# Last layer of a convolution and Fourier chain: two pairs of images side by side, inverse transform in halves, stores per image

## What is computed

```
z = conv3x3(x, Kj)                    # "conv1"
z = relu(batchnorm(z))                # statistics over all images
z = conv3x3T(z, Kj)                   # "conv2"
x = x + 0.1 * z
x = batchnorm(x)                      # statistics over all images
x = real(ifft2(fft2(x) * t))          # t: a table per channel and frequency
```

## Time and profile before

| | us |
|---|---|
| median of 3 runs | 667.3 (663.94 to 668.04) |
| the profiled execution, its own time | 662.35 |
| its span | 660.5 |

### The profile page before, as it was taken

The page is one execution under the profiler, slowest core; times in us unless marked ns, Lnnn a source line. Parts: engine busy times, 40 slices in busy tenths (PEclk is TensorE's granted clock), DMA queues, the critical chain, the costliest instruction groups (busy, mean ns, idle before and its releaser), DMA issues.

```text
span 660.5 us, 14557 instructions
## 1 busy us (share of the span) xinstructions
PE 616.0 (93%) x5848; PEld 196.2 (30%) x5848; DVE 499.6 (76%) x946; ACT 300.8 (46%) x518; POOL 236.7 (36%) x183
## 2 busy tenths in 40 slices
PE   6598999989999999999999999999999999999883
PEld 4122333322323232223232222333322223333331
DVE  3679888876588877668887967689879676887674
...
GB/s 188 192 167 123 34 34 25 24 53 66 218 52 2 1 66 66 66 193 174 2 1 63 5 73 87 229 110 1 1 66 66 66 108 216 2 1 2 0 66 191
DMA packets 44466, 51.21 MB, mean 78 GB/s; under 512 B 36208, under 2 KB 36336, under 8 KB 42352
## 3 DMA queue, kind: packets, MB, share of 16 engines
...
## 4 chain that ended last, share of the span: by engine, by line
PE 82%; DVE 10%; issue 3%; ACT 1%; DMA 1%; SPq 1%; POOL 0%; DVEq 0%; ACTq 0%; POOLq 0%
PE psum L1124 47%; PE psum L1201 7%; PE psum L1274 5%; PE psum L1348 5%; PE psum L1305 4%; PE psum L1333 3%; DVE work L1025 3%; PE psum L1152 2%; PE psum L1330 2%; PE psum L1189 2%; PE psum L1232 1%; PE psum L1234 1%; DVE work L852 1%; DVE work L1060 1%; DVE spare L852 1%
## 5 line engine op out<-in xcount | busy, mean ns | idle before, releaser
L1124 PE MATMUL psum<-Z,wts 128*32 128x512 f32 x1536 | 173.2, 595 | 0.0
L1124 PE MATMUL psum<-X,wts 128*32 128x512 f32 x1536 | 171.9, 594 | 0.1
L493 POOL TENSOR_TENSOR Z<-X 128x512 f32<-128x512 f32 x64 | 81.9, 1303 | 219.2 <-DVE X L1001 218.1
L584 ACT ACTIVATE Z<-psum 128x512 f32<-128x512 f32 x64 | 38.1, 595 | 114.9 <-PE psum L1124 103.8
L512 POOL TENSOR_TENSOR X<-Z 128x1024 f32<-128x1024 f32 x24 | 57.0, 2398 | 88.2 <-DVE Z L1042 88.2
L648 ACT ACTIVATE Z<-Z,small 128x512 f32<-128x512 f32 (+4 forms) x92 | 80.3, 922 | 4.5 <-DVE small L964 4.0
L1124 PEld LDWEIGHTS psum<-X,wts 128*32 128x32 f32 x1536 | 46.5, 109 | 113.7 <-issue 110.2
L1124 PEld LDWEIGHTS psum<-Z,wts 128*32 128x32 f32 x1536 | 45.7, 109 | 112.6 <-issue 111.0
L870 DVE BATCH_NORM_STATS2 stats<-Z 128x6 f32<-128x512 f32 x60 | 41.1, 689 | 43.6 <-ACT Z L584 43.2
L669 ACT ACTIVATE work<-X,small 128x512 bf16<-128x512 f32 x64 | 45.5, 713 | 59.1 <-DVE X L1001 59.1
L1001 DVE SCALAR_TENSOR_TENSOR X<-psum,X 128x512 f32<-128x512 f32 x64 | 43.6, 682 | 24.1 <-PE psum L1124 22.7
...
## 6 DMA issues: line engine op xcount, KB each, us to landing
...
```

The source lines that it names most:

```text
L493: nc.gpsimd.tensor_tensor(rows(Z0, REG, bp, CH * (2 * half + i), CH), low, high, op=op)\
L1124: last = nc.tensor.matmul(out_b[C * r:C * r + C, :], weights[:, o:o + C], rows(src, reg, bp, g, CH, dj - 1), start=(dj == 0), stop=(dj == ...
```

## The change

It has four parts.

1. In the last layer, the `fwdW` of pair 2 is no longer done behind `conv2` chunk 14. It stands in the tail, right before the `fwdW` of pair 3, and then both pairs pass `slot0`, `fwdH`, `invH` one after the other, each step of pair 2 followed by the same step of pair 3, instead of pair 3 following pair 2 at a distance. The `invW` and `back` of pair 1 come first in the tail, ahead of `moments`. Pair 3 gets buffers of its own for `turned`, `freqw` and `spec`, cut out of X2, which nobody reads any more by then.
2. `invH` of pairs 0 to 2 of the last layer is done in halves as in the other layers (with weights of their own, 128 more columns in `cst`, 64 KB), and POOL does `unmix_halves` for them; `affine` reads its result from X0. Pair 3 keeps the dense form.
3. A store is one DMA per image and half of a pair, from all 128 partitions, 256 KB, issued after each half's `affine`, for pairs 0 to 2. Pair 3: also one DMA per image and half. 16 DMAs in all where there were 20.
4. `affine` of pairs 0 and 1 comes after `slot0c` of pair 3; `affine` of pair 2 waits for POOL, and stands ahead of `affine` of pair 3 in ACT's order.

```diff
@@ -44,7 +44,9 @@
 C_STACK = C_MASK + 2
 C_QUAD = C_STACK + C
 C_FH = C_QUAD + R
-C_ALL = C_FH + 64
+C_IB = C_FH + 64
+C_ALL = C_IB + 128
+BY_HALVES = 3
 P_K = 0
 P_F = P_K + 2 * TAPS * C
...
@@ -137,7 +139,7 @@
         11: fourier(j, 1, "fwdH") + [("slot0c", j, 1)],
         12: fourier(j, 0, "invW") + [("back", j, 0, 0), ("back", j, 0, 1)],
         13: fourier(j, 1, "invH"),
-        14: fourier(j, 2, "fwdW"),
+        14: fourier(j, 2, "fwdW") if j + 1 < DEPTH else [],
     }
     for c in range(NCH):
         steps.append(("conv2", j, c))
...
@@ -171,12 +173,14 @@
 def last_steps(j):
-    steps = [("slot0", j, 2)] + fourier(j, 2, "fwdH") + [("slot0c", j, 2), ("moments", j)]
-    steps += [("turn", j, BP - 1, 0), ("turn", j, BP - 1, 1), ("norm", j, 2), ("affine", j, 0)] + fourier(j, 3, "fwdW")
-    steps += fourier(j, 2, "invH") + [("slot0", j, 3)] + fourier(j, 3, "fwdH") + [("slot0c", j, 3)]
-    steps += fourier(j, 1, "invW") + [("back", j, 1, 0), ("back", j, 1, 1), ("affine", j, 1)]
-    steps += fourier(j, 2, "invW") + [("back", j, 2, 0), ("back", j, 2, 1)] + fourier(j, 3, "invH") + fourier(j, 3, "invW")
-    return steps + [("affine", j, 2), ("back", j, 3, 0), ("back", j, 3, 1), ("affine", j, 3)]
+    steps = fourier(j, 1, "invW") + [("back", j, 1, 0), ("back", j, 1, 1), ("moments", j)]
+    steps += [("turn", j, BP - 1, 0), ("turn", j, BP - 1, 1)] + fourier(j, 2, "fwdW") + fourier(j, 3, "fwdW") + [("norm", j, 2)]
+    for bp in (2, 3):
+        steps += [("slot0", j, bp)] + fourier(j, bp, "fwdH") + [("slot0c", j, bp)]
+    steps += [("affine", j, 0), ("affine", j, 1)] + fourier(j, 2, "invH") + fourier(j, 3, "invH")
+    for bp in (2, 3):
+        steps += fourier(j, bp, "invW") + [("back", j, bp, 0), ("back", j, bp, 1), ("affine", j, bp)]
+    return steps
 SUMS = {c: (c,) for c in range(3)} | {4: (3,), 6: (4,), 9: (5, 6), 10: (7, 8), 11: (9,), 12: (10, 11), 13: (12, 13), 14: (14,), 15: (15,)}
...
@@ -352,6 +356,21 @@
                 return pool_slot[pool_product(c, dj, r) % POOL_SLOTS]
             return dve_slot[dve_product(c, dj, r) % DVE_SLOTS]
+        def beside(j, bp, t, i):
+
+            return X2[:, WORK * i:WORK * (i + 1)] if (j, bp) == (DEPTH - 1, BP - 1) else t[:, :]
+
+        def rows_of(j, bp):
+            return beside(j, bp, freqw, 0)
+
+        def spectrum(j, bp):
+            return beside(j, bp, spec, 1)
+
+        def turned_half(j, bp, half):
+            if (j, bp) == (DEPTH - 1, BP - 1):
+                return X2[:, 2 * WORK + 2 * N * half:2 * WORK + 2 * N * (half + 1)]
+            return turned[(2 * bp + half) % 3]
+
         block = ctx.enter_context(nc.Block())
         class Bank:
...
@@ -394,12 +413,17 @@
                     to = lines(t, reg, bp, a, b - a, 0, C * q, C * q + C).rearrange("p (g b) w -> p b g w", b=2)
                     eng.dma_start(to[:, b2], in_dram(x_in, 2 * bp + b2, r)[:, a + dg:b + dg]).then_inc(done, 16)
-        def store(eng, bp, l, n):
-
-            for q in range(R):
-                to = out[2 * bp:2 * bp + 2].rearrange("i c (q l) w -> q c i (l w)", q=R)[q]
-                both = Z2[C * q:C * q + C, bp * REG2:bp * REG2 + 2 * G * W].rearrange("p (i x) -> p i x", i=2)
-                eng.dma_start(to[:, :, W * l:W * l + W * n], both[:, :, W * l:W * l + W * n]).then_inc(out_done, 16)
+        def store(eng, bp, h, first=0, n=G):
+
+            for b2 in range(2):
+                if bp < BY_HALVES:
+                    to = out[2 * bp + b2].rearrange("c (h q l) w -> h q c (l w)", h=2, q=R)[h]
+                    o = bp * REG2 + (2 * b2 + h) * 2 * CH * W
+                    eng.dma_start(to, Z2[:, o:o + 2 * CH * W]).then_inc(out_done, 16)
+                else:
+                    to = out[2 * bp + b2].rearrange("c (q l) w -> q c (l w)", q=R)[:, :, W * first:W * (first + n)]
+                    o = bp * REG2 + b2 * G * W + W * first
+                    eng.dma_start(to, Z2[:, o:o + W * n]).then_inc(out_done, 16)
         def shift_two(eng, dst, src, bp, done, h=None):
...
@@ -452,11 +476,12 @@
                     sp.dma_start(parS[:, :], par[j + 1]).then_inc(par_in, 16)
             for bp in range(BP - 1):
-                sp.wait_ge(x_back, NCH * (DEPTH - 1) + Q * bp + Q)
-                store(sp, bp, 0, G)
+                for h in range(2 if bp < BY_HALVES else 1):
+                    sp.wait_ge(x_back, NCH * (DEPTH - 1) + Q * bp + (2 * h + 2 if bp < BY_HALVES else Q))
+                    store(sp, bp, h)
             sp.wait_ge(x_back, NCH * DEPTH - Q + 2)
-            store(sp, BP - 1, 0, G // 2)
-            sp.wait_ge(out_done, 16 * R * (BP + 1))
+            store(sp, BP - 1, 0, 0, G // 2)
+            sp.wait_ge(out_done, 16 * 2 * (BP + 1 + BY_HALVES))
         @block.gpsimd
         def _(pool):
...
@@ -508,7 +533,8 @@
                 pool.wait_ge(x_summed, NCH * j + Q * bp + Q)
                 even, odd = (rows(Z0, REG, bp, 2 * CH * p, 2 * CH).rearrange("p g (b w) -> p g b w", b=2) for p in range(2))
                 for half, op in enumerate((ALU.add, ALU.subtract)):
-                    dst = rows(X0, REG, bp, 2 * CH * half, 2 * CH).rearrange("p g (w b) -> p g b w", b=2)
+                    dst = rows(X0, REG, bp, 2 * CH * half, 2 * CH)
+                    dst = dst.rearrange("p g (b w) -> p g b w" if j == DEPTH - 1 else "p g (w b) -> p g b w", b=2)
                     nc.gpsimd.tensor_tensor(dst, even, odd, op=op).then_inc(parts_added, 1)
             for j in range(DEPTH):
...
@@ -521,7 +547,7 @@
                         mix_halves(j, BP - 1, 1)
                     elif what == "conv2" and at[1] % Q > 1 and (at[1] < NCH - 1 or j == DEPTH - 1):
                         mix_halves(j, at[1] // Q, at[1] % Q - 2)
-                    elif what == "back" and j + 1 < DEPTH and at[2] == 1:
+                    elif what == "back" and (j + 1 < DEPTH or at[1] < BY_HALVES) and at[2] == 1:
                         unmix_halves(*at[:2])
         @block.scalar
...
@@ -683,10 +709,13 @@
                         return
                 for h in range(2):
                     if j == DEPTH - 1:
-                        act.wait_ge(rows_back, 2 * (BP * j + bp) + h + 1)
+                        if bp < BY_HALVES:
+                            act.wait_ge(parts_added, 2 * (BP * j + bp) + h + 1)
+                        else:
+                            act.wait_ge(rows_back, 2 * (BP * j + bp) + h + 1)
                         both = Z2[:, bp * REG2:bp * REG2 + 2 * G * W].rearrange("p (b l w) -> p l b w", b=2, w=W)
                         dst = both[:, 2 * CH * h:2 * CH * h + 2 * CH]
-                        src = rows(Z0, REG, bp, 2 * CH * h, 2 * CH).rearrange("p g (b w) -> p g b w", b=2)
+                        src = rows(X0 if bp < BY_HALVES else Z0, REG, bp, 2 * CH * h, 2 * CH).rearrange("p g (b w) -> p g b w", b=2)
                     else:
                         act.wait_ge(parts_added, 2 * (BP * j + bp) + h + 1)
                         dst = src = rows(X0, REG, bp, 2 * CH * h, 2 * CH)
...
@@ -1325,12 +1354,14 @@
                     bk.result(NUMBER["fwdH", j, c + x])
                 bk.result(NUMBER["slot0c", j, bp])
                 for x in range(2):
-                    src = spec[:, N * (q + x):N * (q + x) + N]
-                    if j == DEPTH - 1:
+                    src = spectrum(j, bp)[:, N * (q + x):N * (q + x) + N]
+                    dense = j == DEPTH - 1 and bp >= BY_HALVES
+                    c_ih = C_IB if j == DEPTH - 1 else C_IH
+                    if dense:
                         last = nc.tensor.matmul(bank(first + x), cm((C_IL, C_IX)[x]), src, start=True, stop=True)
-                    for p in range(2 if j < DEPTH - 1 else 0):
+                    for p in range(0 if dense else 2):
                         k, half = slice(64 * (p ^ x), 64 * (p ^ x) + 64), slice(64 * p, 64 * p + 64)
-                        last = nc.tensor.matmul(bank(first + x)[half], cstS[k, C_IH + 64 * x:C_IH + 64 * x + 64], src[k],
+                        last = nc.tensor.matmul(bank(first + x)[half], cstS[k, c_ih + 64 * x:c_ih + 64 * x + 64], src[k],
                                                 start=True, stop=True, tile_position=(64 * (p ^ x), 64 * p))
                     last.then_inc(filled[(first + x) % BANKS], 1)
```

26 lines of the change are left out of this document (14 added, 12 removed).

## The result

| | before | changed |
|---|---|---|
| median of the runs, us | 665.65 (4 runs, 663.94 to 668.04) | 688.47 (4 runs, 686.20 to 691.69) |
| profiled execution, its own time, us | 662.35 | 691.69 |
| its span, us | 660.5 | 689.9 |

A forecast was written before the change was run, and what follows sets the result against it. PE was taken to bound the kernel up to the last `conv2` chunk, then a ladder of waits; 5.5 us saved there, 6.4 us ahead after the ladder, 1.7 after POOL, 1.0 after the stores: 666.3 us, range 662.3 to 669.2.

The forecast's parts named there:

- The stores: End of the span: last stores flow from 652.75 at 269 GB/s for 5.85 us, so the span ends at 659.5.
- Rival 1: Final stores: DMAs from 128 partitions reach 344 GB/s, span 2.2 to 2.7 us faster than before; chance 0.27.
- rival 2: Tail: PE stays at half clock until about 639, ending 2.1 us slower than before; chance 0.15.
- The first account: PE's work up to the last `conv2` chunk: 5.5 us less, so that chunk ends at 616.5 instead of 622.0.
- The ladder: Tail behind the last `conv2` chunk, DVE and PE in turns: `back` of pair 3 ends at 648.3, 6.4 us ahead.
- What takes it back: End of the tail: ACT waits for POOL's sums of pair 2, ends at 654.35; of 6.4 us, 1.7 are left.

The follow-up runs named there:

- e1: The changed kernel with only its stores put back to four DMAs of 32 partitions, both images in each: 664.26 us, ratio to before 0.9996.
- e10: The changed kernel with its 128-partition stores written to 16 blocks of 8 rows, outermost dimension 16 (rows misplaced, rate test only): 662.69 us.
- e2: The changed kernel with its 128-partition stores written to 128 consecutive rows of 2 KB, outermost dimension 128 (rows misplaced, rate test only): 664.13 us.
- e6: The kernel before with only the constants' array 128 columns (64 KB) longer, read by nobody: 665.50 against 665.59 us, ratio 1.0005.
- e12: e4 with the stores of the dense pair 2 issued by halves: 662.99 us against 665.73 before, ratio 0.9961.
- e4: e1 with pair 2 dense again, only pairs 0 and 1 in halves, without POOL's sums for pair 2: 663.24 us, ratio to before 0.9970.

## Why the prediction was wrong, point by point

**The step that failed is the term "The stores".** It took 269 GB/s, "the nearest in form" to 128 partitions and pieces of 2 KB. The rate was 102. The pieces had the same form, and the row that I took, the last pair of before, had them too; what I did not look at was the outermost dimension, 32 in every row that I priced from and 4 in the change. The words of that term, "Pairs 0 and 1 leave between 636 and 646 in the shadow", failed with it: at 102 GB/s each pair takes 10 us. By the stretches some 1.5 MB had left when ACT ended at 660.90, and 2.7 MB were still to go, where I had less than 1.57. I laid 5.15 us between ACT's end and the end of the span (659.5 - 654.35); it was 29.0. The difference, 23.9 us, is what lies between the forecast (1.0 us faster) and the result (22.8 us slower by the medians). In e1, where the stores have the old form, the span ends 5.9 us behind ACT.

**The rivals.** None had it. Rival 1 asked only whether wide stores are faster, and they are, once 16 engines carry them: 327 GB/s in e10, 378 in e2. How many engines carry them is another question, and the change had altered that. The figure of the Trainium skill, "SBUF — State Buffer", section "Door 1: The DMA port swizzle", that the prediction weighed, 328 GB/s for 1 MiB over all 128 partitions, is near e10's 327; e2 went beyond it, and the changed kernel's 102, also from 128 partitions, is no case of it. The rival that was missing reads: a DMA is cut up by its outermost dimension, and this one's is 4. No row of before could price it. That is the warning: the whole output was to leave in a form of DMA that the trace did not contain, and I bounded it by rows of other forms. The range had a smaller fault of its own: it was said to take in rival 2, which is at 669.4, and ended at 669.2.

**The first account held.** Halves take 1.95 us on PE, dense 3.70, and `fwdW` of pair 2 left. From the start of `invH` of pair 0 to the end of the last chunk there were 28.0 us before (622.01 - 594.00) and 22.45 in the changed kernel (622.85 - 600.40): 5.6 us less, 5.5 predicted. That the changed kernel's last chunk still ended at 622.85 and not at 616.5 is the start of the execution: its `invH` of pair 0 began 6.4 us later than in the profile of before, while up to there only the constants differ, and e6 shows that these cost nothing measurable. With the same constants it began at 596.40 in e1 and at 594.47 in e12, so single executions are some 6 us apart at this point, whatever the change. The rows themselves:

```profile
600.40 1.95 PE L1364 MATMUL psum<-work,cstS 64*64 64x512 f32 x16
...
615.62 1.95 PE L1364 MATMUL psum<-work,cstS 64*64 64x512 f32 x16
```

**The ladder held as a sum.** From the last chunk to ACT's end I laid out 654.35 - 616.5 = 37.85 us. Measured: 38.05 in the changed kernel (660.90 - 622.85), 37.94 in e1 (656.80 - 618.86). Inside, two errors of e1 cancelled:

```profile
632.68 0.22 DVE L1078 TENSOR_TENSOR work<-psum,tabT 128x64 f32<-128x64 f32 x1
...
636.50 1.26 DVE L1089 TENSOR_TENSOR X<-psum,tabT 128x496 f32<-128x496 f32 x2 [1.15 <-PE psum L1334]
```

The norm was done at 632.7, 13.8 us behind the last chunk where I had 15.1 (631.6 - 616.5), since `fwdW` of pair 3 still ran at full clock. Then DVE waited 1.15 and 0.30 us in the middle of scaling pair 3, for a `fwdH` at half clock. In the changed kernel the clock was low at another point, `fwdW` itself (3.72 us), and the sum came out alike: `move_slots` starts 20.5 us behind the last chunk (643.33 - 622.85), 20.4 in e1 (639.23 - 618.86) and in my layout (636.9 - 616.5).

**Rival 2 took place in part.** The granted clock was 0.50 from 630 to 638 in the changed kernel (the row of 636 to 638 above), and `fwdW` of pair 3 took 3.72 us instead of some 2. But the rival turned on whether the clock is back when `invH` of pair 2 starts, and it was, at 641.6:

```profile
638.00:640.00 2.00, 1.76 (x22) 1.11 (x22) 1.93 (x7) 0.28 (x1) 0.00 (x0) 0.75 0.00 0
640.00:644.00 4.00, 4.00 (x41) 1.62 (x38) 4.00 (x9) 2.05 (x3) 0.00 (x0) 1.00 0.01 4
```

I priced a low clock until 639 at 3.1 us. What the shorter one cost can be read from e4, where the clock was low from about 631 to 638, and e12, where it stayed at 1.00: 35.1 - 32.8 = 2.3 us from last chunk to ACT's end, from one execution of each. The layout's 37.85 us met executions with a low clock; by that difference they would be an estimated 2.3 us too long for one like e12's.

**What takes it back held.** POOL's sums of pair 2 begin as soon as the fourth of the eight `back` is done, ACT waits for them twice (8.36 and 1.08 us of idle time before its rows), and pair 3, ready at 654.9, is scaled from 658.5 on. e4 takes the sums away, and ACT ends 2.8 us sooner.

**The size of what is left.** With working stores the forecast was 1.0 us faster. e1 is 1.0 us below before by the medians, and 0.9996 by the ratio, which can't tell it from nothing. So nothing contradicts the rest of the sum, but a gain of 1.0 us isn't shown by it.
